# Cutting the last two stores of a streamed kernel into uneven pieces of partitions, and moving its row of indices to partition 127

## The reference: what is computed

```python
B, C, D, T, N_SUBJECTS = (128, 128, 128, 1024, 8)
w = weights[subjects]
out = jnp.einsum('bct,bcd->bdt', x, w)
x = x + out
```

## Time and profile before

| | |
|---|---|
| median of 3 runs | 325.82 us (325.64 to 326.04) |
| the profiled execution's own time | 326.13 us |
| its span, from first to last instruction | 324.2 us |
| busy PE, DVE, POOL, ACT | 238.1, 238.5, 201.5, 70.4 us |
| bytes moved | 134.82 MB, mean 416 GB/s |
| loads: issue to landing, median | 18.6 us |
| stores: issue to landing, median | 31.5 us |

### The profile page before, as it was taken

One profiled execution on the slowest core, in us unless ns is written; L12 is line 12 of the kernel. 1 busy time (PEld: TensorE's weight loads), 2 busy tenths in 40 slices (PEclk: granted clock), 3 DMA queues, 4 the chain that ended last, 5 costly groups with the idle time before them and its releaser, 6 DMA issues.

```text
span 324.2 us, 4021 instructions
## 1 busy us (share of the span) xinstructions
PE 238.1 (73%) x1024; PEld 106.2 (33%) x1024; DVE 238.5 (74%) x208; ACT 70.4 (22%) x81; POOL 201.5 (62%) x197
## 2 busy tenths in 40 slices
PE   0599999999977877876867768768677687686700
PEld 0244444444433333332332323323233233233300
DVE  3089999999987787686776876867768768677630
ACT  5122322222222112122122121221221212212200
POOL 0377878888875665665755756657557566574320
PEclk9999999999999999999999999999999999999975
DMA  7999999999999999999999999999999999999993
GB/s 284 425 409 415 424 428 423 430 425 428 426 428 428 425 432 425 428 427 427 428 426 431 425 429 426 427 428 425 432 425 429 426 429 426 428 429 422 430 426 165
DMA packets 18968, 134.82 MB, mean 416 GB/s; under 512 B 2065, under 2 KB 2578, under 8 KB 2578
## 3 DMA queue, kind: packets, MB, share of 16 engines
q1 hardware_dynamic: 9744, 67.64, 49.8%
q10 hardware_dynamic: 9218, 67.11, 49.0%
HBM read 67.63 MB, written 67.11 MB: 416 GB/s over the span
## 4 chain that ended last, share of the span: by engine, by line
DMA 63%; PE 28%; ACT 2%; issue 1%; DVE 1%; POOLq 0%; DVEq 0%; ACTq 0%; POOL 0%; SPq 0%
DMA out<-x_ring 39%; PE product L189 28%; DMA x_ring<-x 23%; DMA weight_halves<-weights 1%; ACT weight_bank L130 1%; ACT weight_bank L131 1%; POOLq L154 0%; DVEq L37 0%; DVE x_ring L91 0%; DVE x_ring L89 0%; ACTq L116 0%; POOL weight_ring L155 0%; SPq L71 0%; ACT crossed L111 0%; POOLq L155 0%
## 5 line engine op out<-in xcount | busy, mean ns | idle before, releaser
L189 PE MATMUL product<-x_ring,weight_ring 64*128 64x512 f32 x1024 | 238.1, 603 | 68.9 <-DMA x_ring<-x 55.3
L161 POOL TENSOR_TENSOR x_ring<-crossed,x_ring 64x1024 f32<-64x1024 f32 x64 | 150.6, 2352 | 90.5 <-ACT crossed L111 90.5
L189 PEld LDWEIGHTS product<-x_ring,weight_ring 64*128 64x128 f32 x1024 | 106.2, 188 | 200.1 <-issue 192.4
L89 DVE TENSOR_TENSOR x_ring<-product,x_ring 64x1024 f32<-64x1024 f32 x64 | 77.9, 1217 | 65.7 <-PE product L189 64.5
L111 ACT COPY crossed<-product 64x1024 f32<-64x1024 f32 x64 | 64.3, 1004 | 234.2 <-PE product L189 209.7
L90 DVE TENSOR_TENSOR x_ring<-product,x_ring 64x1024 f32<-64x1024 f32 x64 | 78.6, 1228 | 0.8
L91 DVE TENSOR_TENSOR x_ring<-product,x_ring 64x1024 f32<-64x1024 f32 x64 | 78.5, 1226 | 0.9
L155 POOL COPY weight_ring<-weight_bank 64x256 f32 x128 | 50.8, 396 | 18.3 <-issue 12.2
L98 DVE COPY weight_bank<-weight_halves 64x128 f32<-64x128 f32 x8 | 1.8, 219 | 4.8 <-DMA weight_halves<-weights 4.7
L130 ACT COPY weight_bank<-weight_halves 64x128 f32<-64x128 f32 x8 | 2.4, 303 | 2.0 <-DMA weight_halves<-weights 2.0
L131 ACT COPY weight_bank<-weight_halves 64x128 f32<-64x128 f32 x8 | 2.4, 299 | 0.1
## 6 DMA issues: line engine op xcount, KB each, us to landing
x_ring<-x SPq DMA_DIRECT2D x64, 1024.0 KB, 18.6
out<-x_ring ACTq DMA_DIRECT2D x64, 1024.0 KB, 31.5
weight_halves<-weights SPq DMA_DIRECT2D x1, 512.0 KB, 3.9
subject_row<-subjects ACTq DMA_DIRECT2D x1, 0.5 KB
```

The source lines that it names most:

```text
L89: dve.tensor_tensor(x_ring[LOW, slot, 0, :], low[LOW, :], x_ring[LOW, slot, 0, :], add)
L161: pool.tensor_tensor(x_ring[HIGH, slot, 1, :], crossed[HIGH, slot % 2, :], x_ring[HIGH, slot, 1, :], add).then_inc(joined, 1)
L189: last = pe.matmul(product[slot % PRODUCTS][a][:, cols], weight_ring[half, slot, r, :], x_ring[half, slot, r, cols], start=r == 0, stop=r ...
```

## The change

The store of tile 62 becomes three DMAs, of partitions 0 to 63, 64 to 123 and 124 to 127. The store of tile 63 becomes two, of partitions 0 to 119 and 120 to 127. All other stores stay whole. The waits at the end count 16 for each piece. The row of subject numbers lies on partition 127 in place of partition 0, and the reads of it follow.

```diff
+PIECES = {-2: ((0, 64), (64, 124), (124, 128)), -1: ((0, 120), (120, 128))}
...
-        subject_row = ctx.enter_context(nc.sbuf_tensor("subject_row", [1, B], i32))
+        subject_row = ctx.enter_context(nc.sbuf_tensor("subject_row", [C, B], i32))
...
-            def store(tile, slot):
+            def store(tile, slot, pieces=((0, C),)):
                 act.wait_ge(summed, tile + (PRODUCTS + 1))
                 act.wait_ge(joined, tile + 1)
-                act.dma_start(out_of_tile[bass.ds(tile, 1)], x_ring[:, slot, :, :]).then_inc(x_out[slot], DMA_INC)
+                for begin, end in pieces:
+                    act.dma_start(out_of_tile[bass.ds(tile, 1), begin:end, :],
+                                  x_ring[begin:end, slot, :, :]).then_inc(x_out[slot], DMA_INC)
...
-            act.dma_start(subject_row[0:1, :], subjects.rearrange("(one b) -> one b", one=1)).then_inc(subjects_in, DMA_INC)
+            act.dma_start(subject_row[C - 1:C, :], subjects.rearrange("(one b) -> one b", one=1)).then_inc(subjects_in, DMA_INC)
...
             for slot in range(REST):
-                step(LAPS * SLOTS + slot, slot)
-            store(TILES - 1, REST - 1)
+                step(LAPS * SLOTS + slot, slot, PIECES.get(slot - 1 - REST, ((0, C),)))
+            store(TILES - 1, REST - 1, PIECES[-1])
             for slot in range(SLOTS):
-                act.wait_ge(x_out[slot], DMA_INC * (LAPS + (slot < REST)))
+                last_pieces = len(PIECES.get(slot - REST, (0,))) if slot < REST else 0
+                act.wait_ge(x_out[slot], DMA_INC * (LAPS + last_pieces))
...
-                    subject = pool.value_load(subject_row[0:1, bass.ds(tile * 2 + a, 1)], min_val=0, max_val=S - 1)
+                    subject = pool.value_load(subject_row[C - 1:C, bass.ds(tile * 2 + a, 1)], min_val=0, max_val=S - 1)
```

More of the change, by code:

```diff
@@ L111, in cross, with step @@
                 act.copy(crossed[HIGH, slot % 2, :], product[slot % PRODUCTS][1][LOW, :]).then_inc(copied, 1)
-            def store(tile, slot):
+            def store(tile, slot, pieces=((0, C),)):
                 act.wait_ge(summed, tile + (PRODUCTS + 1))
                 act.wait_ge(joined, tile + 1)
-                act.dma_start(out_of_tile[bass.ds(tile, 1)], x_ring[:, slot, :, :]).then_inc(x_out[slot], DMA_INC)
-            def step(tile, slot):
+                for begin, end in pieces:
+                    act.dma_start(out_of_tile[bass.ds(tile, 1), begin:end, :],
+                                  x_ring[begin:end, slot, :, :]).then_inc(x_out[slot], DMA_INC)
+            def step(tile, slot, pieces=((0, C),)):
                 act.wait_ge(joined, tile - 1)
                 cross(tile, slot)
-                store(tile - 1, (slot - 1) % SLOTS)
-            act.dma_start(subject_row[0:1, :], subjects.rearrange("(one b) -> one b", one=1)).then_inc(subjects_in, DMA_INC)
+                store(tile - 1, (slot - 1) % SLOTS, pieces)
+            act.dma_start(subject_row[C - 1:C, :], subjects.rearrange("(one b) -> one b", one=1)).then_inc(subjects_in, DMA_INC)
             act.sem_inc(copied, PRODUCTS)
```

## The result

The changed kernel takes 329.79 us (median of 4 runs, 328.11 to 330.46) against 325.93 us for the one before (325.64 to 326.12). The ratio is 1.0108, with a 95% interval of 1.0082 to 1.0134: about 1.1% slower, where 0.8% faster was predicted. It also scatters more, 2.4 us where the kernel before has 0.5. The profiled execution took 329.43 us with a span of 327.6.

A forecast was written before the change was run, and what follows sets the result against it. DMA transfers were taken to bound the kernel, with one late engine alone at the end; moving that end from 323.1 to 320.4 saved 2.7 us, with zero charged for other parts: 325.82 - 2.7 = 323.1 us, range 322.3 to 326.7.

The forecast's parts named there:

- Where the kernel is bound: Whole kernel: transfers set the time at about 427 GB/s; one engine alone works at the end, perfect balance worth 3.95 us.
- the row's new place: Subject row on partition 127: reads might double from 0.344 us; charged zero, upper bound 0.5 us.
- Which engine is late: Tail: the late engine serves the subject row's partition, two reads a tile making 0.075 us of lag.
- late engine: 323.1 - 12 x 0.307 = 319.4: Last two stores: the late engine carries twelve rows fewer, so it ends at 319.4 us in place of 323.1.
- rival B: Tail: the late engine is not the one relieved; 325.8 to 326.4 us, chance 0.14.
- among the others: Branch where the unrelieved late engine is not one of the first four: 325.8 to 326.1 us.
- The engine shares: Last two stores: pieces of 60 and 120 partitions leave out the last engine; end moves to 320.4, 2.7 us less.
- A row costs 0.307 us: Tail stores: one 8 KB row takes an engine 0.307 us, used to price rows gained or lost.
- rival A: Pieces: each SBUF partition group gives one engine's rate, so engines sharing it slow down; 326.8 us, chance 0.22.
- 5.1 us on the bulk: Engines other than the late one: from 319.0, plus 2.4, 1.6 and about 1.0, given as ending at 324.1 us.
- A's signs: Signs of shared partition groups: a share below 1 before 318 us, or 0.6 us rows while tile 62 is stored.
- B's: Sign of the wrong engine relieved: a stretch at share 0.06 of 3 us or more, ending at 323 or later.

The follow-up runs named there:

- e5: Kernel before with its last two stores each cut in two along the free dimension, all 128 partitions in each DMA: 325.78 us, ratio 0.9996.
- e1: Kernel before with only the subject row moved to partition 127, all stores whole: 325.82 us, ratio 1.0001.
- e3: Kernel before without reads of subject numbers, each pick taking a matrix fixed by its slot: 325.58 us, ratio 0.9997.
- e8: Kernel before with tile 63's store cut into 112, 7, 6 and 3 partitions: 326.18 us, one run.
- e12: Kernel before with tile 63's store cut into 112, 5, 5, 5 and 1 partitions: 326.85 us, one run.
- e7: Kernel before, followed by five separated stages of stores: whole tiles, lower halves, halves in turn, partitions 0 to 119, partitions 120 to 127: 432.71 us.
- e11: Kernel before with tiles 62 and 63 each stored as 112 and four times 4 partitions: 328.82 us, ratio 1.0089.
- e4: Kernel before with its last two stores each cut into halves of 64 partitions: 327.67 us, ratio 1.0068.
- e17: Kernel before, followed by a two-queue mix of whole loads and stores with 1440 matmuls looping beside it: 926.67 us, one run.
- e9: Kernel before, followed by 96 whole transfers, half loads and half stores, on two queues without compute: 564.63 us, one run.
- e16: Kernel before with all arithmetic cut to 8 columns, waits, loops and transfers kept: 324.83 us, one run.
- e14: Kernel before with the laps written out on SP and ACT alone: 325.52 us, ratio 0.999.
- e15: Kernel before with the laps written out on VectorE, GpSimd and TensorE alone: 325.44 us, ratio 0.9989.
- e10: Kernel before, followed by 96 whole transfers without compute, load and store in turn on one queue: 567.27 us, one run.

## Why the prediction was wrong

**Where the kernel is bound: right.** The transfers set the end, two more issues cost nothing (e5), the row's new place costs nothing (e1), and the tail of one engine is real.

**Which engine is late: wrong, and this is the step that failed first.** "I take it to be the engine that serves the row's partition" rested on a count (two reads a tile) and on two times that were close together. e3 took the reads away and the lag stayed; e1 moved the row and nothing else moved; e8, e12 and the changed kernel's own tail put it at the fifth engine. So the term "late engine: 323.1 - 12 x 0.307 = 319.4" had the wrong sign: it has one row more, + 0.3 us. That is rival B, in its branch of "among the others", 325.8 to 326.1 us.

**The engine shares: right in number, wrong in what they cost.** 15, 15, 4 and 8 engines took part. But "A row costs 0.307 us" holds only while no two engines are at one group of partitions: in e7 a row of a half takes twice that. That is rival A. It was priced on the wrong engines, though: it put 5.1 us on the bulk (its own terms add up to 324.0 and not 324.1) and let the relieved engine off. The second latest engine's last landing came at 322.76 us, against 320.44 before, so 2.3 us; and that did not set the end. The loss that counts fell on the late engine, 3.2 us in tile 61, a store that the change does not touch. The likely reason is that it was still at older rows in its own group when engines ahead of it came there for theirs.

**The size.** The term said 319.4 us for the late engine's last packet and the trace says 326.6. Of these 7.2 us, 4.0 are the thirteen rows between twelve fewer and one more, and 3.2 are the eight rows of tile 61. A and B were given 0.22 and 0.14 and treated as alternatives, the one at 326.8 and the other at 325.8 to 326.4 us. Both hold at once, and neither alone gives the measured time. The sum that the runs show is 323.1 + 3.2 + 0.3 = 326.6 us for the last packet, 3.5 us later than before; the profiled execution took 329.43 us, 3.3 more than before, and the median moved by 3.9, to 329.79 where 323.1 was forecast. Relieving the late engine would not have been enough: in e11 it has two rows fewer and still loses 3.6 us in tile 61.

**What would show it.** Both of A's signs came: a share of 0.90 from 316 to 318 us, and rows of 0.6 us and more while tile 62 is stored (e4 against e5 for the reason). The share is the weaker sign. From 314 to 316 us it stood at 1.02 while the rate was down to 360 GB/s: an engine that waits for its group counts as busy. B's came as it stands, a stretch at 0.06 of 3.6 us that ends past 323. PE's pace stayed about what it was: from 271.72 to 301.49 us it starts six tiles, 4.96 us each.

**Still open.** Why the fifth engine falls behind. What the runs show, mostly by one execution each, is that past 1.4 us it grows with running compute engines (e17 against e9), and without the reads (e3), large operands (e16) or the loops of SP and ACT (e14). With the compute engines' laps written out, it stands out less from the others (e15). Whether it is how instructions are fetched, or something else that goes with executing them, was not told apart. Nor is it shown directly that the late engine's group of partitions is the one where the others met it; the 5.6 us for eight rows in a whole store, 4.5 in e4, and e5, in which no such meeting exists and the loss is gone, are the grounds for it.

## What to carry to other kernels

Before rows are taken off a late DMA engine, find out which it is: a store in pieces over known numbers of engines leaves its mark in the late engine's last completions. A cut across partitions also changes which engine reads where, and here it slowed the engine that was still at older, whole stores, most likely by meeting it in its group; the cut along the free dimension (e5) did neither. And when two rivals touch the same engine, price them together.

## What the runs showed of the hardware that was not expected

* Stores of 64 partitions run at 209 GB/s with all sixteen engines at a share of 1.00, against 426 for 128 partitions (e7; e4 from 308 to 314 us). A row takes 0.63 us in them and 1.25 us in stores of partitions 120 to 127, against 0.31. A busy share says nothing of the rate when engines meet.
* One DMA engine of sixteen, the fifth if the first k engines get the shares, falls behind by 0.07 us a tile in the kernel before (1.10 us at tile 12, 4.36 at tile 60). With transfers alone the lag of the latest engine stops at 1.4 us (e9: 1.35 us at 449 us and 1.36 at 538).
* On one queue the same mix keeps the latest engine within 0.55 us of the median, and on two queues within 1.4 (e10, e9; one execution each).
